# Experts' rows weighted and scattered to their tokens inside the experts' stage, and read back by plain DMA in layer 1

## The reference, cut to what matters

```python
def _L0_ffn_ref(x, w12, w3, gate_w):
    scores = jnp.einsum('btd,ed->bte', x, gate_w)
    topk_scores, topk_idx = jax.lax.top_k(scores, TOP_K)
    topk_probs = jax.nn.softmax(topk_scores, axis=-1)
    total_probs = jnp.sum(jax.nn.one_hot(topk_idx, E, dtype=topk_probs.dtype) * topk_probs[..., None], axis=-2)
    h1, h2 = (h12[..., :H], h12[..., H:])
    hidden = jax.nn.silu(h1) * h2
    expert_out = jnp.einsum('bteh,edh->bted', hidden, w3)
    y = jnp.sum(total_probs[..., None] * expert_out, axis=-2)
...
x = x + _L0_xattn_ref(_layernorm(x, axis=-1), ctx_1024)
x = x + _L0_ffn_ref(_layernorm(x, axis=-1), L0_ffn_w12, L0_ffn_w3, L0_ffn_gate_w)
x = x + _L1_xattn_ref(_layernorm(x, axis=-1), ctx_1024, ctx_1024, mask_BxS_bk1)
x = x + _L1_ffn_ref(_layernorm(x, axis=-1), L1_ffn_w1, L1_ffn_b1, L1_ffn_w2, L1_ffn_b2)
```

## Time and profile before

| what | us |
|---|---|
| median of 3 runs (lowest, highest) | 721.78 (719.36, 723.9) |
| the profiled execution: its time | 723.95 |
| its span, first to last instruction | 722.0 |
| busy: PE, DVE, ACT, POOL | 563.3, 528.6, 368.1, 365.0 |
| expert blocks, first up to last copy of a result | 162.0 to 463.5 |
| first layer-1 DMA | 465.6 |
| first and last masking of scores in layer 1 | 496.2, 582.2 |
| first GELU | 597.8 |

### The profile page before, as it was taken

One profiled execution on the slowest core, in us unless ns is written; L12 is line 12 of the kernel. 1 busy time (PEld: TensorE's weight loads), 2 busy tenths in 40 slices (PEclk: granted clock), 3 DMA queues, 4 the chain that ended last, 5 costly groups with the idle time before them and its releaser, 6 DMA issues. The chain is left out here.

```text
span 722.0 us, 17429 instructions
## 1 busy us (share of the span) xinstructions
PE 563.3 (78%) x5923; PEld 487.9 (68%) x5923; DVE 528.6 (73%) x1494; ACT 368.1 (51%) x715; POOL 365.0 (51%) x387
## 2 busy tenths in 40 slices
PE   4687955009999999999999999505668747899996
PEld 3566844008999999999999999504545523565665
DVE  6887776805866766667655655239989997999997
ACT  2499743003343443443433443204676629999994
POOL 1015275779999999998000000177773226544440
PEclk9778755559999999999999999855667979999999
DMA  5998242422222222223222222294565200011112
GB/s 196 367 356 303 62 153 79 150 90 48 61 70 65 61 69 65 62 67 68 60 68 68 60 68 67 69 340 118 171 189 158 75 1 0 16 38 38 37 39 73
DMA packets 77588, 74.80 MB, mean 104 GB/s; under 512 B 44480, under 2 KB 67904, under 8 KB 76224
## 3 DMA queue, kind: packets, MB, share of 16 engines
q1 hardware_dynamic: 71360, 56.92, 25.4%
q0 software_dynamic: 6144, 16.79, 7.3%
HBM read 40.51 MB, written 23.86 MB: 89 GB/s over the span
## 5 line engine op out<-in xcount | busy, mean ns | idle before, releaser
L906 PE MATMUL banks<-z_turned,w_of_block 128*128 128x128 f16 x3408 | 203.7, 220 | 32.9 <-DMA z_turned<-z_rows 32.9
L906 PEld LDWEIGHTS banks<-z_turned,w_of_block 128*128 128x128 f16 x3408 | 191.8, 98 | 36.1 <-issue 33.0
L994 DVE SCALAR_TENSOR_TENSOR hidden_T<-banks,blk_inv,silu_T 128x512 f32<-128x512 f32 x71 | 53.3, 751 | 117.4 <-PE banks L906 95.8
L1192 POOL DMA_INDIRECT expert_rows_in<-expert_rows,places_of_rows x64 | 64.0, 999 | 144.0 <-POOLq L1023 125.0
L403 POOL DMA_INDIRECT z_rows<-z_parts,places_in_regions x64 | 64.5, 1008 | 88.8 <-DVE places_in_regions L716 70.5
L959 ACT ACTIVATE hidden_T_high<-hidden_T 128x512 fp32r<-128x512 f32 x71 | 44.9, 632 | 109.1 <-DVE hidden_T L994 109.1
L986 DVE COPY w_of_block<-w_parts 128x4096 f16 x71 | 94.2, 1328 | 3.9 <-issue 3.9
L919 PE MATMUL banks<-w_low,hidden_T_high 128*128 x284 | 85.8, 302 | 2.8 <-DVE hidden_T_low L1000 2.7
L952 ACT ACTIVATE silu_T<-banks,blk_inv 128x512 f32<-128x512 f32 x71 | 48.8, 688 | 67.0 <-PE banks L906 66.9
L919 PE MATMUL banks<-w_high,hidden_T_high 128*128 x284 | 79.6, 280 | 0.0
L919 PE MATMUL banks<-w_high,hidden_T_low 128*128 x284 | 79.3, 279 | 0.0
(11 more groups left out here) (240 smaller groups left out, 1307.7 us busy)
## 6 DMA issues: line engine op xcount, KB each, us to landing
expert_rows<-expert_out SPq DMA_DIRECT2D x71, 128.0 KB, 1.7
w_parts<-in_w SPq DMA_DIRECT2D x7, 1024.0 KB, 7.2
x_rows<-in_x SPq DMA_DIRECT2D x8, 512.0 KB, 6.2
c_T<-in_ctx_turned SPq DMA_DIRECT2D x16, 256.0 KB, 4.1
w_low<-in_w SPq DMA_DIRECT2D x8, 512.0 KB, 8.8
c_T_in<-in_ctx_turned SPq DMA_DIRECT2D x32, 128.0 KB, 2.3
c_in<-in_ctx_rows SPq DMA_DIRECT2D x32, 128.0 KB, 3.1
out<-rows_out SPq DMA_DIRECT2D x32, 128.0 KB, 1.7
```

Source lines behind the costliest of these rows:

```text
L906: mm = pe.matmul(PS[:, 1 + half + 2 * u, hc * P:(hc + 1) * P], win[:, u, wp, c, at:at + P], zturn[:, j % ZB, k, :], start=(n == 0), stop=( ...
L994: v.scalar_tensor_tensor(out=g[:, :], in0=PS[:, 2 + 2 * u, :], scalar=blk_inv[:, j:j + 1], in1=s[:, :], op0=ALU.mult, op1=ALU.mult).then_i ...
L1192: pool.indirect_dma_start(rows[:, k, n, :], None, y_rows[:, :], bass.IndirectOffsetOnAxis(ap=place[:, R * i + k, n:n + 1], axis=0))\
```

## The change

Each row in `z_rows` gets 16 bytes more (`told`): the number of its token, its expert codes and the exponential of its score gap. SP loads these for each block (`load_told`), DVE makes from them for eight blocks at a time the weight of each row and the row of its token in a new HBM tensor `token_rows` (`weigh`). ACT applies the weight when it copies the result. Blocks 0 to 63 are stored to `y_rows` as before; from its iteration 49 on SP fetches them back to SBUF, up to three in an iteration, and GpSimd scatters them to `token_rows` (`hand_out`); the last seven are scattered from `ye` itself. Each of these steps has its waits: `fetch(j)` for the scatter of block j - 8, `keep_y(j)` of the last blocks for the scatter of block j - 2.

In layer 1 SP loads the two rows of each token by plain DMA (`load_rows`), and GpSimd adds both to `X1`. b1's parts are made on a 128x8 tile and laid out through HBM. The weights of the feed-forward part are loaded in quarters and treated by ACT in groups 2 and 3 (k = 0, 1 and 6, 7 of group 2; 0, 1 of group 3). The norms of the last part are done in four chains of 8 tiles, three of them in groups 2, 3 and the last passes, as are the first eight `largest_x` and the first `scale_x`; TensorE starts the feed-forward part without waiting for the last sums. `h_rounded` has four buffers, and the last four tiles are rounded at once. The core of the diff:

```diff
 Z_ROWS = SPARE + (E - 1) * P
 ZP = 14
+ZW = 2 * D + 8
+PAD = NB * P
+TOKENS = PAD + 2 * T * P
+DIRECT = NB - 7
+WEIGH = 7
...
                 def scatter(t):
 
                     pool.wait_ge(put, PUT * (route_of[t] + 1))
                     pool.wait_ge(zl_made, t + 1)
+                    pool.wait_ge(told_put, pieces_done[route_of[t]])
                     for k in range(2):
                         pool.indirect_dma_start(z_rows[:, :], bass.IndirectOffsetOnAxis(ap=put_at[:, t, k:k + 1], axis=0),
                                                 zp[:, t % ZP, :], None).then_inc(scattered[t % ZP], 16)
...
+                def exp_gaps(r):
+                    t0, t1 = ROUTES[r]
+                    act.wait_ge(picked, PICK * (r + 1))
+                    a.activation(told[:, t0:t1, 2], dl[:, t0:t1], ACT.Exp).then_inc(exped, 1)
...
                     assert ch.n == PUT
+                    dve.wait_ge(exped, r + 1)
+                    for p0, p1 in pieces[r]:
+                        slots = slice(p0 % ZP, p0 % ZP + p1 - p0)
+                        v.tensor_copy(zp[:, slots, D:ZW // 2].bitcast(F32), told[:, p0:p1, :]).then_inc(told_put, 1)
 
...
+                def load_told(j):
+                    sp.dma_start(told_in[:, j, :], z_rows[bass.ds(rows[j], P), D:ZW // 2].bitcast(F32)).then_inc(told_got, 16)
+
+                def fetch(j):
+
+                    if j == 0:
+                        sp.wait_ge(w_ready, E)
+                    k = j % NQ
+                    sp.wait_ge(ye_out[j % 2], 16 * (j // 2 + 1))
+                    after(sp, moved_out[k], MOVED[k] + 16 * (j // NQ) if j >= NQ else 0)
+                    sp.dma_start(stage[:, k, :], y_rows[j * P:(j + 1) * P, :]).then_inc(staged[k], 16)
...
                 def store(j):
                     u = j % 2
+                    if j >= DIRECT:
+                        return
                     sp.wait_ge(ye_made, j + 1)
                     sp.dma_start(y_rows[j * P:(j + 1) * P, :], ye[:, u, :]).then_inc(ye_out[u], 16)
...
                 sp.wait_ge(tables, TABLES)
                 for j in range(NB):
                     if j % READ == 0:
                         rows += block_values(mybir.EngineType.SP, blk_row, j, Z_ROWS - P)
                     load(j)
+                    if j % READ == 0:
+
+                        after(sp, weighed, WEIGH * (j // READ))
+                        for n in range(j, min(j + READ, NB)):
+                            load_told(n)
                     if j >= ZB - 1:
                         store(j - ZB + 1)
-                for j in range(NB - ZB + 1, NB):
-                    store(j)
-                sp.wait_ge(ye_out[0], 16 * (NB // 2 + 1))
-                sp.wait_ge(ye_out[1], 16 * (NB // 2))
+                    if j >= FETCH0:
+                        for _ in range(3):
+                            if fetched < min(j - ZB - 1, DIRECT):
+                                fetch(fetched)
+                                fetched += 1
+                for j in range(fetched, DIRECT):
+                    fetch(j)
 
...
+                def hand_out(j):
+
+                    pool.wait_ge(weighed, WEIGH * (j // READ + 1))
+                    to = bass.IndirectOffsetOnAxis(ap=dest[:, j:j + 1], axis=0)
+                    if j < DIRECT:
+                        k = j % NQ
+                        pool.wait_ge(staged[k], 16 * (j // NQ) + 32)
+                        pool.indirect_dma_start(token_rows[:, :], to, stage[:, k, :], None).then_inc(moved_out[k], 16)
+                    else:
+                        pool.wait_ge(ye_made, j + 1)
+                        pool.indirect_dma_start(token_rows[:, :], to, ye[:, j % 2, :], None).then_inc(moved_out[j % NQ], 16)
+
                 for e in range(1, E):
                     prepare(e)
+                for j in range(NB):
+                    hand_out(j)
+                for k in range(NQ):
...
                 def keep_y(j, u):
-                    after(act, ye_out[u], 8 * (j - u))
+                    if j - 2 < DIRECT:
+                        after(act, ye_out[u], 8 * (j - u))
+                    else:
+                        act.wait_ge(moved_out[(j - 2) % NQ], MOVED[(j - 2) % NQ] + 16 * ((j - 2) // NQ) + 16)
+                    act.wait_ge(weighed, WEIGH * (j // READ + 1))
                     act.wait_ge(yo_made, j + 1)
-                    a.activation(ye[:, u, :], PS[:, 6 + u, 0:D], ACT.Copy).then_inc(ye_made, 1)
+                    a.activation(ye[:, u, :], PS[:, 6 + u, 0:D], ACT.Copy, scale=weight[:, j:j + 1]).then_inc(ye_made, 1)
 
                 act.wait_ge(tables, TABLES)
...
+                def weigh(b):
+                    cols = slice(READ * b, min(READ * b + READ, NB))
+                    n = cols.stop - cols.start
+                    ch = Chain(dve, weighed, WEIGH * b)
+                    dve.wait_ge(told_got, 16 * cols.stop)
+                    ch.post(v.tensor_tensor(hit[:, 0:n], told_in[:, cols, 1], blk_code[:, cols], ALU.is_equal))
+                    ch.link(v.tensor_scalar(share[:, 0:n], told_in[:, cols, 2], 1.0, None, ALU.add))
+                    ch.post(v.scalar_tensor_tensor(out=aim[:, 0:n], in0=hit[:, 0:n], scalar=-float(T * P),
+                                                   in1=told_in[:, cols, 0], op0=ALU.mult, op1=ALU.add))
+                    ch.post(v.reciprocal(share[:, 0:n], share[:, 0:n]))
+                    ch.link(v.tensor_tensor(hit[:, 0:n], hit[:, 0:n], told_in[:, cols, 2], ALU.max))
+                    ch.post(v.tensor_tensor(dest[:, cols], aim[:, 0:n], spill[:, cols], ALU.max))
+                    ch.link(v.tensor_tensor(weight[:, cols], hit[:, 0:n], share[:, 0:n], ALU.mult))
+                    assert ch.n == WEIGH
...
+                    if (j + 2) % READ == 0 and j + 2 < NB:
+                        weigh((j + 2) // READ)
 
...
-                def load(i, k):
-
-                    after(sp, o_made, R * i + (k - (R - 1)))
-                    sp.dma_start(cTs[:, k, :], ctd[:, at(i, k), :]).then_inc(c_in[k], 16)
...
+                def load_rows(t):
+                    after(sp, x2_made, t - (R - 1))
+                    sp.dma_start(rows[:, t % R, :, :], by_token[:, t, :, :]).then_inc(r_in[t % R], 16)
+
+                def load(t):
+
+                    after(sp, o_made, t - (R - 1))
+                    sp.dma_start(cTs[:, t % R, :], ctd[:, t:t + 1, :]).then_inc(c_in[t % R], 16)
+                    sp.dma_start(cs[:, t % R, :], cd[:, t:t + 1, :]).then_inc(c_in[t % R], 16)
+
+                def load_w(n, part):
+                    cols = slice(part * 512, (part + 1) * 512)
+                    sp.dma_start(wst[:, n, cols], (w1, w2)[n].rearrange("p c w -> p (c w)")[:, cols]).then_inc(w_in[n], 16)
+
+                sp.dma_start(b1c[:, :], b1.rearrange("(p c) -> p c", c=F // P)).then_inc(b1_moved, 16)
+                for t in range(Q):
+                    load_rows(t)
+                for t in range(R):
+                    load(t)
+                    if t + Q < R:
+                        load_rows(t + Q)
+                for t in range(Q):
+                    load_rows(R + t)
+                sp.wait_ge(b3_made, 2)
+                sp.dma_start(b1_rows.rearrange("r (p c) -> p r c", c=F // P), bhl[:, :, :].bitcast(F32)).then_inc(b1_moved, 16)
                 sp.dma_start(b2b[:, :], b2.partition_broadcast(P)).then_inc(b_in, 16)
-                for n, w in enumerate((w1, w2)):
-                    sp.dma_start(wst[:, n, :], w.rearrange("p c w -> p (c w)")).then_inc(w_in[n], 16)
-                for i in range(1, NR):
-                    for k in range(R):
-                        load(i, k)
+                for t in range(R, T):
+                    if t + Q < T:
+                        load_rows(t + Q)
+                    load(t)
+                    if t < 2 * R:
+                        load_w(t // 4 % 2, t % 4)
+                    if t == 2 * R:
...
             def _(pool):
-                def gathers(i):
-                    for k in range(R):
-                        after(pool, r_in[k], 32 * i)
-                        after(pool, x2_made, R * (i - 1) + (k + 1))
-                        for n in range(2):
-                            pool.indirect_dma_start(rows[:, k, n, :], None, y_rows[:, :],
-                                                    bass.IndirectOffsetOnAxis(ap=place[:, R * i + k, n:n + 1], axis=0))\
-                                .then_inc(r_in[k], 16)
-
-                gathers(0)
+                def sum_first(t):
+                    pool.wait_ge(r_in[t % R], 16 * (t // R) + 16)
+                    pool.tensor_tensor(X1[:, t, :], X1[:, t, :], rows[:, t % R, 0, :], ALU.add).then_inc(x2_half, 1)
+
+                def sum_second(t):
+                    pool.wait_ge(x2_half, t + 1)
+                    pool.tensor_tensor(X1[:, t, :], X1[:, t, :], rows[:, t % R, 1, :], ALU.add).then_inc(x2_made, 1)
+
```

(55 more changed lines are left out.)

235 lines of the change are left out of this document (105 added, 130 removed).

## The result

The changed kernel takes 775.86 us (772.58 to 776.96, 4 runs) where the kernel before took 722.84 beside it: the ratio is 1.0732, 95% interval 1.0678 to 1.0787. The profiled execution has a span of 770.7 us against 722.0, so 48.7 us are to be found.

A forecast was written before the change was run, and what follows sets the result against it. TensorE bounds the experts, DVE layer 1's attention and the feed-forward part, with gaps at the seams between stages. Terms 0.5 + 13 - 12.3 + 8.2 - 9 + 1 = +1.4 us on the median 721.78 give 723 (705 to 741).

The forecast's parts named there:

- Scatters and the wait ahead of block 66: Experts' end: GpSimd scatters spaced 1.48 us make ACT's copy of block 66 14.7 us late; the hand-out sums to +13.
- The reason given for a scatter's loss: Experts: a scatter under a DVE copy needs DVE's release about 0.13 us before its end; a copy costs 0.59 us.
- I charge nothing: Experts: fetches on SP ahead of z loads and stores cost 0, some 5 us of lateness covered; up to 3 otherwise.
- The end of the experts: Last copy to layer 1: a scatter's landing of 2.4 us replaces the store's 1.7, so +0.7 us.
- Start of layer 1: Barrier to first neg_scores: about 18.3 us against 30.6, so -12.3 us (-9 to -15).
- The 1.5 us allowed for GpSimd beside the chain: Start of layer 1: some 1.5 us added to the norm chain's 4.2 for GpSimd working beside it.
- Attention: Layer 1, first to last neg_scores: 94.2 us against 86.0, so +8.2 us (-2 to +18).
- held links: Attention: 47 GpSimd sums cost DVE 14.1 us; as slower rival, each holds DVE its whole length, 743 us, chance 0.15.
- with rows up to tile 11 already asked for: Attention: SP stands behind `b3_made` at the start, but rows up to tile 11 are already requested; no cost given.
- Feed-forward part: After attention: last product to first GELU about 1.6 us instead of 10.3, -9; rounding four tiles at once +1 (0 to 3.3).
- the long stall: Slower rival, experts: each DVE copy keeps a scatter out its whole length, spacing 1.80 us, total 735 us; chance 0.19.

The follow-up runs named there:

- the last pair: Changed kernel with layer 1's rows asked for three tiles earlier, and the changed kernel itself, on one chip: 810.98 and 813.56 us (kernel before 759.58).
- the run with the early start alone: Kernel before with only the last norms in four chains and TensorE's first up not waiting for the last sums: ratio 1.0052.

## Why the prediction was wrong

It said 723 (705 to 741) and the time is 776. Against the forecast of each stretch the largest misses are 12.9 us in blocks 46 to 65, 9.7 behind the first GELU and 8.4 at the end of the experts. Point by point:

- **Scatters and the wait ahead of block 66: right in size.** Spacing 1.48 by instruction as worked out, 1.56 with waits for fetched rows; copy 65 to 70 +10.9 for +12.3. The chain of steps was off in its parts: the first scatter was at 371.9 for 367.4, block 64's at 471.61 for 460.1, and no time was caught up from 66 to 70 (15.2 us for 11.6). The copies behind 66 waited for no scatter there: TensorE stood until 477.98, 8.15 us in all, and then ran the downs and ups of a block at its lower clock (the ups took 4.04 us for 2.85, the granted clock from copy 66 to 70 is 0.70), for which the prediction had 1 us. That TensorE was late itself when the wait began kept the total near the forecast; that is luck. The reason given for a scatter's loss is wrong in one number: most ended 0.82 us behind the copy (374.54 + 1.91 against 374.41 + 1.22), not 0.13, as one row under two copies had suggested. That the mean came out as worked out, although most were held longer than assumed, is in part luck too.
- **"I charge nothing" for SP's lateness: the step that failed first, 12.9 us.** The step asked whether a z load lands in time if SP is late once, and covered that by buffers. It didn't add up SP's issue time over an iteration, and it counted the told loads as cheap where they start, not where they meet the fetches. The trace of before had the times for it: 0.33 us for an issue, times eight told loads, three fetches and a store, and 1.2 for a turning load make over 5 us in one iteration, against 4.17. Of the 12.9, SP's part is 9.5 and the scatters' 3.4. It holds for the first chip; on the chip of the last pair this stretch lost 40 us and more, mostly by something else.
- **The end of the experts: 0.7 predicted, 9.1 measured.** No step priced what it means that GpSimd, idle since 341 us in the kernel before, now works up to the barrier. Nothing in the trace of before shows it, and no bound was put on it.
- **Start of layer 1: right in kind, -7.3 for -12.3.** GpSimd's sums ran at 0.68 us from start to start and held DVE's links of tile 0's chain at the same pace (0.65 to 0.77 us each, at 511.6 to 515.0 and 517.3 to 520.0). With DVE's own sums the same loads give -12.7. The 1.5 us allowed for GpSimd beside the chain should have been some 5.
- **Attention: +12.5 for +8.2, inside its bounds, by luck.** The held links were priced too high: 8.8 us for 14.1, with 41 of GpSimd's sums in the stretch and not 47, at 0.2 us each and not 0.3. What made the stretch long is a term that the sum put at nothing: 12.5 us go when the rows are asked for earlier, and the 86.7 that are left are below the 94.2 of the forecast. The sentence "with rows up to tile 11 already asked for" looked at the first group only. The tiles beyond were the row to follow: which load stands ahead of which on SP, and when its buffer is free.
- **Feed-forward part: -9 + 1 predicted, -2.4 + 10.7 measured.** The first GELU was to be 1.6 us behind the last add_out and was 5.3 (630.10 + 0.48 to 635.83). In the run with the early start alone the same place shows why: ACT loads a table (1.28 us), then TensorE has its up and b1 matmuls at the lower clock (1.91 and 1.41 us, 591.57 to 594.33). And the early chain costs the attention 4.8 us, 3.9 of them in the one sum that GpSimd's `centre` held. By itself this part of the change is a loss of half a per cent. The thin b1 matmuls, 6 us, were in the diff and in no step.
- **The rivals.** Of the slower ones the long stall came nearest (its wait is there, at 1.48 us a scatter), the held links were there at 0.2 us a sum. Neither gives 776: four mechanisms that had no step (SP's burst, GpSimd at the barrier, late rows, thin matmuls) make 9.5 + 9.1 + 12.5 + 6 = 37 of the 48.7.

## What to carry over

Before a queue gets more DMAs, add up the issue times of everything it does in one period, bursts included, against the period: here 3.5 of 4.17 us left no room for eight loads of 0.5 to 0.7. Follow each moved load to the wait that stands ahead of it on its queue, and ask when that one is released, in the middle of the loop and not at its start. An engine that starts to work in the last microseconds ahead of a barrier, or a matmul that shrinks in rows, is a change of its own and wants a step in the sum, if only with a bound.

## What the runs showed of the hardware that was not expected

- With the b1 matmuls on 3 rows TensorE's clock is mostly at 1.2 GHz in a stretch in which the engine is busy 8 of 10 us (0.54 and 0.56), and at 2.4 GHz with the same program on 128 rows, 125 of them zero (1.00). The Trainium skill (TensorE: Matmul & The Clock Gate, Why this matters for your kernels) has it that a single matmul on few rows saves no time. The shortest of the 64 agree (383 ns in the changed kernel, 387 before), but from the start of one of a tile's two to the start of the next it is 0.33 to 0.35 us on 3 rows and 0.42 on 128 at the upper clock, so they save 0.08 us and lose far more by the clock.
- GpSimd instructions that follow each other without a gap can hold one DVE instruction for more than one of them: 4.36 us for a sum of 0.48 beside seven `centre`, 2.06 for a link of 0.17 beside two memsets. Small links mostly got through one to a GpSimd instruction (0.65 to 0.77 us each beside sums at 0.68).
- A GpSimd scatter that lies under a DVE copy ends behind it, by 0.82 us (14 of 19) or 0.12 (5 of 19).
- A stage in which GpSimd issued a DMA near its end ended 5.8 us (one scatter, landed at 461.18, the last store at 461.60, next DMA at 467.00) and 6.5 us (seven, 475.13 and 481.61) after that DMA had landed, with every engine silent; after a memset the end came 1.2 us later than without.
- Chips differ: 721 to 723 us for the kernel before on four occasions, 760 to 763 on three. Where, two kernels show that differ only in who clears b1's tiles, one on each kind of chip: the first copy of a result is at 170.4 and 188.1, the start of layer 1 takes 31.7 and 46.2 us and the attention 82.3 and 90.7, but blocks 46 to 65 take 79.2 on both.
